# Second attention of a two-layer transformer kernel: both row normalisations as one ScalarE activation each, in place of two GpSimd operations each

## What is computed

```
x = x + L0_xattn(layernorm(x), ctx)      # one head, 512 wide, softmax over 120 rows
x = x + L0_ffn(layernorm(x))             # rows and weights rounded to int8, scaled back
x = x + L1_xattn(layernorm(x), ctx)      # 16 heads of 32, softmax, product with w_o
x = x + L1_ffn(layernorm(x))             # shared expert 1024 wide + 8 experts 256 wide, top 4 of a router

def _layernorm(x, axis=-1, eps=1e-05):
    m = jnp.mean(x, axis=axis, keepdims=True)
    v = jnp.var(x, axis=axis, keepdims=True)
    return (x - m) / jnp.sqrt(v + eps)
```

## Time and profile before

| | us |
|---|---|
| median of 3 timed runs | 1249.32 |
| lowest and highest of them | 1249.26, 1250.52 |
| the profiled execution: span from its first to its last instruction | 1257.6 |
| PE (TensorE) busy | 1189.3 |
| DVE (VectorE) busy | 950.4 |
| ACT (ScalarE) busy | 708.7 |
| POOL (GpSimd) busy | 589.7 |

### The profile page before, as it was taken

The page is one execution under the profiler, slowest core; times in us unless marked ns, Lnnn a source line. Parts: engine busy times, 40 slices in busy tenths (PEclk is TensorE's granted clock), DMA queues, the critical chain, the costliest instruction groups (busy, mean ns, idle before and its releaser), DMA issues.

```text
span 1257.6 us, 29419 instructions
## 1 busy us (share of the span) xinstructions
PE 1189.3 (95%) x10692; PEld 822.8 (65%) x10692; DVE 950.4 (76%) x2006; ACT 708.7 (56%) x1988; POOL 589.7 (47%) x685
## 2 busy tenths in 40 slices
PE   6888998799999999999999999999999998799996
PEld 3555665588888888786444445777777776466663
DVE  5889898899999999896677777777777775445460
ACT  4377788799899999896344322222222231365552
POOL 0047668737666667733200000445544345466744
PEclk9999999999999999999999999999999999899999
DMA  9522033134445454643870141221314320799987
GB/s 346 210 60 76 1 32 46 43 111 142 165 135 169 159 172 148 181 157 119 153 196 1 41 127 34 68 44 60 69 34 108 96 68 2 220 254 242 256 139 96
DMA packets 157567, 150.28 MB, mean 119 GB/s; under 512 B 78544, under 2 KB 111472, under 8 KB 157424
## 3 DMA queue, kind: packets, MB, share of 16 engines
q1 hardware_dynamic: 139584, 125.94, 35.5%
q0 software_dynamic: 13248, 21.15, 8.9%
q10 hardware_dynamic: 4592, 1.32, 0.6%
HBM read 84.93 MB, written 57.19 MB: 113 GB/s over the span
## 4 chain that ended last, share of the span: by engine, by line
PE 59%; DMA 17%; issue 8%; DVE 8%; POOL 5%; ACT 3%; ACTq 0%; SPq 0%; POOLq 0%; DVEq 0%
PE bank L121 28%; DMA lists<-att_land 14%; PE bank L1503 6%; PE bank L2125 5%; PE bank L955 4%; POOL lists L1629 4%; PE bank L1435 4%; PE bank L1456 3%; PE bank L1450 2%; PE bank L1421 2%; DMA q_rows<-att_land 1%; PE bank L1024 1%; ACT att_land L1353 1%; PE bank L872 1%; PE bank L891 1%
## 5 line engine op out<-in xcount | busy, mean ns | idle before, releaser
L1629 POOL DMA_INDIRECT lists<-att_land x128 | 134.4, 1050 | 310.7 <-DVE att_land L1770 166.8
L1353 ACT ACTIVATE att_land<-bank,att_land 128x120 f32<-128x120 f32 x512 | 178.3, 375 | 11.3 <-DVE att_land L1221 11.2
L2125 PE MATMUL bank<-att_land 128*128 128x512 f16 x768 | 177.3, 381 | 0.6 <-DVE program_logits L1304 0.6
L1952 ACT ACTIVATE att_land<-program_x 128x512 f32<-128x512 f32 x40 | 25.2, 631 | 195.2 <-DVE program_x L2094 165.1
L2125 PEld LDWEIGHTS bank<-att_land 128*128 128x128 f16 x768 | 75.4, 98 | 82.9 <-issue 2.0
L121 PE MATMUL bank<-program_xs,program_wgu 128*128 128x512 f16 x576 | 128.7, 379 | 0.6 <-DVE att_land L1729 0.6
L1353 ACT ACTIVATION_READ_ACCUMULATOR att_land<-bank,att_land 128x1 f32 x512 | 112.8, 221 | 0.0
L121 PE MATMUL bank<-att_land 128*128 128x128 f16 (+1 forms) x1560 | 101.0, 221 | 0.5 <-DVE att_land L1278 0.5
L121 PEld LDWEIGHTS bank<-program_xs,program_wgu 128*128 128x128 f16 x576 | 56.2, 98 | 67.5 <-DVE att_land L1729 1.1
L1221 DVE TENSOR_REDUCE att_land<-bank 128x4 f32<-128x480 f32 x128 | 82.4, 644 | 20.5 <-PE bank L1421 20.1
L1503 PE MATMUL bank<-att_land 128*128 128x512 f16 x384 | 93.4, 379 | 0.0
(11 more groups left out here) (305 smaller groups left out, 2817.2 us busy)
## 6 DMA issues: line engine op xcount, KB each, us to landing
att_land<-q_rows SPq DMA_DIRECT2D x96, 128.0 KB, 2.6
xn_rows<-att_land SPq DMA_DIRECT2D x37, 256.0 KB, 3.7
out_rows<-att_land SPq DMA_DIRECT2D x37, 256.0 KB, 6.4
q_rows<-att_land SPq DMA_DIRECT2D x32, 256.0 KB, 2.9
xt_tiles<-att_land SPq DMA_DIRECT2D x32, 256.0 KB, 2.1
x_rows<-program_x SPq DMA_DIRECT2D x8, 1024.0 KB, 4.8
att_land<-x_rows SPq DMA_DIRECT2D x8, 1024.0 KB, 5.6
program_xs<-xt_tiles SPq DMA_DIRECT2D x28, 256.0 KB
```

The costliest lines, as they stand in the source:

```text
L1353: last = act.activation(prob[:, c, h, :], ps_s[c % 2][:, h, :], ACT.Exp, bias=nmax[:, u % 2, c, h:h + 1], accum_out=rsum[:, u % 2, n:n + 1])
L1629: pool.indirect_dma_start(out=io["lists"], out_offset=bass.IndirectOffsetOnAxis(ap=index[:, t, k:k + 1], axis=0), in_=load[:, t, k, :], in ...
L2125: last = pe.matmul(ps_y[i][:, :], hid[:, c % 2, a, i * P:(i + 1) * P], wd[:, q, c, :], start=c == 0 and n == 0, stop=c == NC - 1 and n == 2)
```

## The change

A normalised row is x * rstd + (-mean * rstd). GpSimd now computes the second term for each row, one number (`shift`), right behind the inverse root, and one ScalarE activation (Identity with a scale and a bias by row) makes the whole 128x512 tile from x. The two GpSimd operations on the tile are gone. The b activation (`rows_normalised`) stands on ScalarE behind the exponentials of block 2, so at the end of a step; the g activation (`gate_normalised`) at the end of the step's first part, ahead of the second probability copy. The waits that stood before GpSimd's operations (for the readers of the buffer: the transposes, and for g the write to DRAM two tiles back) now stand on ScalarE. Tiles 0 to 4 of b stay on VectorE. The lists of TensorE, VectorE and SyncE are the same as before.

```diff
 class Norm:
-    def __init__(self, m, name, xn):
+    def __init__(self, m, name, xn, shift, first):
...
     def inverse_root(self, pool, g, u, d):
...
         pool.tensor_tensor(self.rstd[:, d], self.ve[:, d], g.half[:, :], ALU.pow).then_inc(self.root, 1)
+        if u < self.first:
+            return
+        pool.wait_ge(self.root, u + 1)
+        pool.tensor_scalar(self.shift[:, d], self.mv[:, d, 0:1], self.rstd[:, d], -1.0, ALU.mult,
+                           ALU.mult).then_inc(self.shifted, 1)
+
+    def normalise(self, act, g, u):
+
+        act.wait_ge(self.shifted, u + 1 - self.first)
+        act.activation(self.xn[:, u % 2], g.x[:, u, :], ACT.Identity, scale=self.rstd[:, u % 4],
+                       bias=self.shift[:, u % 4]).then_inc(self.ok, 1)
...
     def gpsimd(pool):
-        def apply(norm, mean, u):
-            i = u % 4
-            pool.wait_ge(norm.root, u + 1)
-            pool.tensor_tensor(norm.xn[:, u % 2], g.x[:, u, :], norm.mv[:, i, 0:1].to_broadcast([P, D]),
-                               ALU.subtract).then_inc(mean, 1)
-            pool.wait_ge(mean, u + 1 - (HEAD if norm is ln else 0))
-            pool.tensor_tensor(norm.xn[:, u % 2], norm.xn[:, u % 2], norm.rstd[:, i].to_broadcast([P, D]),
-                               ALU.mult).then_inc(norm.ok, 1)
-
         def step(t):
             u = t - 4
             if live(u):
                 lg.inverse_root(pool, g, u, u % 4)
-                need(pool, rows_out[u % 2], 16 * (u // 2))
-                need(pool, s["g_tr"], u - 1)
-                apply(lg, s["mean_g"], u)
             yield
             u = t + 4
             if live(u):
                 ln.inverse_root(pool, g, u, u % 4)
-            u = t + 3
-            if live(u) and u >= HEAD:
-                if u == HEAD:
-                    pool.wait_ge(ln.ok, HEAD)
-                need(pool, s["xt_mm"], u - 1)
-                apply(ln, s["mean"], u)
...
+        def rows_normalised(u):
+            if live(u) and u >= HEAD:
+                if u == HEAD:
+                    act.wait_ge(ln.ok, HEAD)
+                need(act, s["xt_mm"], u - 1)
+                ln.normalise(act, g, u)
+
+        def gate_normalised(u):
+            if live(u):
+                need(act, rows_out[u % 2], 16 * (u // 2))
+                need(act, s["g_tr"], u - 1)
+                lg.normalise(act, g, u)
+
         def step(t):
             prob_high(t - 1, 0)
             query_high(t + 1)
             rows_high(t + 2)
+            gate_normalised(t - 4)
             yield
             prob_high(t - 1, 1)
             exps(t - 1, 3)
...
             exps(t, 2)
+            rows_normalised(t + 3)
```

More of the change, by code:

```diff
@@ L148 @@
 class Norm:
-    def __init__(self, m, name, xn):
-        self.xn = xn
+    def __init__(self, m, name, xn, shift, first):
+        self.xn, self.shift, self.first = xn, shift, first
         self.st = m.sb(name + "_st", [P, 4, 6])
@@ L156, in __init__ @@
         self.rstd = m.sb(name + "_rstd", [P, 4, 1])
-        self.stats, self.aggr, self.var, self.root, self.ok = (
-            m.sem(f"{name}_{n}") for n in ("stats", "aggr", "var", "root", "ok"))
+        self.stats, self.aggr, self.var, self.root, self.shifted, self.ok = (
+            m.sem(f"{name}_{n}") for n in ("stats", "aggr", "var", "root", "shifted", "ok"))
     def before(self, dve, u, read=None):
@@ L1087, in attention1 @@
     HEAD = 5
[L1088 removed]
+    ln = Norm(m, "b", g.early(0, [P, 2, D]), g.early(SM + 168, [P, 4, 1]), HEAD)
     xT = g.early(2 * D, [P, 2, 2, KC, P], f16)
@@ L1097, in attention1 @@
     oT = g.early(5 * D, [P, 2, 2, KC, P], f16)
-    lg = Norm(m, "g", g.late(5 * D, [P, 2, D]))
+    lg = Norm(m, "g", g.late(5 * D, [P, 2, D]), g.early(SM + 172, [P, 4, 1]), 0)
     gT = g.late(7 * D, [P, 2, 2, KC, P], f16)
```

5 lines of the change are left out of this document (2 added, 3 removed).

## The result

The changed kernel takes **1255.69 us** (median of 18 runs, 1252.33 to 1259.16), the kernel before took 1251.8 us in the runs beside it (median of 18, 1248.09 to 1255.38). The ratio is **1.0031, interval 1.0019 to 1.0043**: 3.9 us slower (2.4 to 5.4), where +1.1 had been predicted. On another chip the same two kernels gave 1.0035 (1.001 to 1.006). The forecast had put the time itself at 1250.4 us, within 1248.0 to 1255.0, from a kernel before of 1249.32. Of the 5.3 us between 1250.4 and 1255.69, 2.5 belong to the kernel before, which took 1251.8 here, and 2.8 to the change, which cost 3.9 and not 1.1.

The account below looks back on a forecast made before the run. TensorE was taken to bound full steps at 10.71 us. Terms 0.8+0.5+1.3-1.6 = +1.0, plus 0.1, gave +1.1 us: span 1258.7, less 8.3 to the timed median, 1250.4 us, range 1248.0 to 1255.0, "within" at 0.66.

Parts of the forecast that it names:

- What bounds the kernel, and where to look: Full steps of the second attention: TensorE sets 10.71 us, GpSimd's work is worth nothing; ask whether ScalarE still fits.
- Rival C: Faster: relief of VectorE counts, at both ends and perhaps in TensorE's transfer waits; 1246.4 us, chance 0.06.
- Rival D: ScalarE stands in line behind a transfer, the row writes of two steps before; near 1250.4 us or slower, chance 0.01.
- ScalarE's step, 10.67 against 10.71: Full step: ScalarE's 9.26 us grows by 1.41 to 10.67, fitting under TensorE's 10.71 by a few hundredths.
- rival A: Slower: full steps become ScalarE's if two activations need over 1.45 us; 0.22 a step, 1255.4 us, chance 0.12.
- The other count: ScalarE's gaps in a full step, found against pitches such as 0.336 us for exponentials, add to 1.4 us of room.
- The full steps, +0.5: TensorE's load of the b rows comes 0.02 us late in each of 25 steps; bounds 0 and 0.22 a step.
- a step in which ScalarE is held up: One step where ScalarE is held up by transfers that it issues and must catch up: +0.1 us.
- Rival B: Slower: TensorE waits for b rows 0.1 us more each full step, 2.5 us in all; 1252.9 us, chance 0.15.
- The start, +0.8: First b activation: TensorE waits 1.0 us, 0.2 won back at a transfer of queries; bounds 0.5 and 1.0.
- The end, +1.3 and -1.6: Last steps: two g activations where ScalarE leads cost 1.3 us; the last g rows, earlier, save TensorE's 1.6 wait.
- The gate's shift: On GpSimd in full steps: 0.2 to 0.55 us, done by 429.8, before ScalarE arrives at 430.2, so no wait.

Follow-up runs that it names:

- b_early: The change with the b activation ahead of the gate's copy and the third run of exponentials instead of behind it; 1.0006 of the kernel before, full steps 10.785 us.
- load_only: The kernel before with both activations added on ScalarE, output never read, GpSimd still normalising; 1.0018 (+2.2 us), full steps 10.785 us.
- b_only: The change with only the query rows' normalisation (b) on ScalarE, g back on GpSimd; full steps 10.72 us.
- g_only: The change with only the gate rows' normalisation (g) on ScalarE, b back on GpSimd; full steps 10.707 us.
- g_last: The kernel before with a single normalisation on ScalarE, the gate rows of the last tile (31); 0.9987 (0.9972 to 1.0002).
- b_mid: The change with the b activation between the gate's copy and the run of exponentials; 1.0009 of the kernel before, steps 10.71 us four times, then 10.765.
- before_again: The kernel before, unchanged, profiled a second time; second attention 341.43 us from its 36th exponential to its last row transposes.
- load_less: The kernel before with both unread activations added on ScalarE, cut from 512 to 384 columns; 1.0025 (1.0012 to 1.0039), full steps 10.707 us.
- g_last2: Repeat of the kernel before with only the last tile's gate-row normalisation on ScalarE; 0.9992 of the kernel before.
- after_again: The changed kernel once more, unaltered, as the mark for other runs; full steps 10.785 us.
- load_more: The kernel before with unread activations added on ScalarE, the one at b's place done twice, so three a step; full steps 11.47 us.

## Why the prediction was wrong, step by step

**What bounds the kernel, and where to look.** Right. The question was whether ScalarE still fits under TensorE, and GpSimd's relief was worth nothing: VectorE's busy time in a full step is 10.21 us in the change and was 10.12. Rival C falls in the full steps. What it rests on did show once, at the end: of the eight VectorE operations of L2041 the one at 603.09 had taken 1.53 us beside GpSimd's work, and with that work gone the mean of the eight fell from 790 to 685 ns (before, after). VectorE was idle for 2.19 us a little behind it, so nothing was gained by that.

```profile
L2041 DVE SCALAR_TENSOR_TENSOR att_land<-att_land 128x512 f16<-128x512 f32 x8 | 6.3, 790 | 0.0
```

```profile
L2049 DVE SCALAR_TENSOR_TENSOR att_land<-att_land 128x512 f16<-128x512 f32 x8 | 5.5, 685 | 0.0
```

Rival D did not show.

**ScalarE's step, 10.67 against 10.71.** This is the step that failed. "A whole step without the gate's copy took 267.52-258.74 = 8.78 us" counts from start to start. The same two rows have durations of 0.67 and 0.77: that step finished at 268.29 and began with a finish at 259.41, which is **8.88 us**. The tenth of a microsecond was the arrears growing, in plain view. With a copy at 0.49 and two activations at 0.70, 8.88+0.49+1.40 = 10.77, over TensorE's 10.71, and the forecast would have been rival A. The ends from the kernel before give the same: 13x0.342+3x0.250+3x0.577+4x0.489 = 8.88. The other count, with exponentials at 0.336, has the same fault, and the rows, where a run of four goes from 0.35 to 0.37 us, show it in small. The text ahead of the prediction says that in a busy stretch the next start is the better measure; along an unbroken run it is not, the end is. What the activation itself costs was right: 0.70 us from finish to finish, as in the earlier trace rows.

**The full steps, +0.5.** They cost 0.06 to 0.08 us each. From the third step to the one at 530 us that is +1.0 us in the two profiles of the change (265.3-27.2 = 238.1 against 262.9-25.8 = 237.1), less than 22 times 0.06 to 0.08, because at each wait for a transfer of queries ScalarE catches up: the step with the first such wait took 11.82 and 11.72 us in the change, 11.98 and 11.83 before. The step at 530 us costs 0.4 more (13.07 and 13.16 against 12.78 and 12.69), where the sum had 0.1 for a step in which ScalarE is held up by transfers; in the first profile TensorE waits 0.28 for the b rows there. Rival B, which had TensorE wait for the b rows, named the place rightly and the mechanism wrongly: b ends 0.07 late since it lasts 0.89 and not 0.82, and b_early and load_only lose the same without that wait. Rival A was the one that held, though not by its own condition, "once the two together need more than 1.45": they need 1.40, as forecast, and the room is 1.3. Its price was wrong as well, 0.22 a step and 5.5 us in all; that its 1255.4 us lies next to the measured 1255.69 is luck, since the full steps cost 1.0 and the kernel before alone ran 2.5 us longer than the forecast had it.

**The start, +0.8.** It was 1.4. The wait at the first b was forecast as 1.0 us and is 1.09:

```profile
271.87 0.66 PE L1464 MATMUL bank<-program_ident,att_land 128*128 128x128 f32 x4 [1.09 <-ACT att_land L191]
```

0.9 of it is left at the next half. I had not seen the two steps behind it: they cost 0.2 and 0.25 more (in b_only the first of these alone), probably since ScalarE, whose first b activation lasts 0.98 us there, had not caught up; no run singles this out. "The other b and g of the start meet gaps" was wrong.

**The end, +1.3 and -1.6.** Near in both: +1.5 from the step at 545 us to the last half (58.8 us against 57.3), where TensorE waits for exponentials 0.61, 0.53 and 0.75 us instead of 0.62 once; and 7.40 instead of 8.77 us behind the last half, -1.4. g_only has both alone, and g_last the second without the first. The last rows of after:

```profile
610.25 0.81 ACT L191 ACTIVATE att_land<-program_x,att_land,attention_g_rstd 128x512 f32<-128x512 f32 x1 [0.45 <-POOL att_land L185]
```

```profile
611.12 0.66 PE L1464 MATMUL bank<-program_ident,att_land 128*128 128x128 f32 x4 [0.21 <-ACT att_land L191]
```

**The sum.** 1.4+1.0+0.4+1.5-1.4 = +2.9 us in the trace, against +1.1. Of the 1.8 that are missing, 0.8 are full steps and the step at 530 us, 0.6 the start and 0.4 the two ends. So the term that failed by its mechanism, the full steps, is not the whole miss. The timed difference is 1.0 more still, with no cause shown. **The gate's shift** was as said: 0.28 us on GpSimd in the mean of the 32, and nobody waits for it in a full step.

The Trainium skill (ScalarE: Activation LUTs, section "What ACT_TABLE_LOAD costs") gives a formula for one activation and has neighbours "overlap by ≈ 93 ns". For 512 columns with scale and bias by row it gives, as an estimate, 186+2x93+427 = 799 ns alone and 706 in a row, which is what the traces have (0.80 to 0.83, and 0.70). For an exponential of 120 columns with one pointer it gives 280+100-93 = 287 ns, an estimate too, and the runs have 0.343 from finish to finish and 0.336 from start to start. The step's total can't be built from it; here the measurement decides.

## What to carry to other kernels

When work is to be put on an engine with a few hundredths to spare, count what it already does from finish to finish, not from start to start: durations that grow along an unbroken run mean that it starts work faster than it ends it, and the growth is part of its time. If a moved instruction's place is in doubt, add its load alone, with no reader: that one run separates "the engine is full" from "the reader waits". If the runs of a kernel fall into two kinds by their granted clock, compare within a kind. And work that is harmless in the steady part may still be worth moving for one instance, here the last one, which alone stood on the path.

## What the runs showed of the hardware

**ScalarE runs ahead of itself.** The same 128x512 activation lasts 0.81 us when nothing stands before it, 0.83 in b_only, 0.89 in the change, and 1.29 in b_mid. The exponentials go from 0.35 to 0.94 us. None of this is work: from end to end the same instructions take 0.70 and 0.342 to 0.343 us in all of these, so what grows is the time between an early start and a finish in turn. The lead grew to 0.5 to 0.6 us in these kernels and then stayed; whether a limit of the engine's own or the work of others stopped it isn't shown.

**The same program has two faces before it reaches the changed code.** The granted clock from 217 to 223 us and from 236 to 248 us was 0.60 and 0.72 in the profile of the change and 1.00 in that of before, and I first took this for part of the loss: the first attention of after runs 5 us longer there than in before. But in the second profile of before it is the same. The stretches of before_again:

```profile
217.00:223.00 6.00, 6.00 (x48) 4.46 (x47) 4.59 (x14) 3.34 (x8) 3.55 (x6) 0.57 0.01 3
236.00:248.00 12.00, 8.95 (x76) 6.27 (x76) 7.49 (x20) 7.44 (x22) 8.10 (x14) 0.72 0.17 55
```

Of the 14 profiles five have both low stretches (before_again, after, b_early, load_less, g_last2). Nine have 1.00 in the first; of these three (after_again, load_only, load_more) are at 0.89 or 0.90 in the second. Of the five, before_again is the kernel before itself, so the face is not the change's doing. A clock of 0.60 over a stretch is a mixture of the two levels, 1.2 and 2.4 GHz. One pair of profiles would have laid 5 us to the change that belong to the execution; the comparison from a common point behind it does not. The timed runs show the same: on one chip, with one kernel, 1244.58 us at a mean granted clock of 0.994 or more and 1248.58 at 0.992 or less.
